# A second mixture of experts: tokens sorted by expert through DRAM, in place of all experts for all tokens

## What is computed

```python
# x = x + _L1_ffn_ref(_layernorm(x), w_gate, w1, w3, w2)
E, H, TOP_K = (8, 256, 2)
xt = x.reshape(-1, embed_dim)
logits = xt @ w_gate
top_logits, sel = jax.lax.top_k(logits, TOP_K)
probs = jax.nn.softmax(top_logits, axis=-1).astype(x.dtype)
h = jax.nn.silu(jnp.einsum('td,edh->eth', xt, w1)) * jnp.einsum('td,edh->eth', xt, w3)
y = jnp.einsum('eth,ehd->etd', h, w2)
yk = y[sel.T, t_idx[None, :], :]
out = jnp.einsum('ktd,tk->td', yk, probs)
```

## Time and profile before

| | |
|---|---|
| median of 3 runs | 2715.28 us (2713.32 to 2717.45) |
| the profiled execution, device time | 2702.93 us |
| its span, first to last instruction | 2701.1 us |
| TensorE busy / its clock, mean | 89% / 0.945 |
| VectorE, ScalarE, GpSimd busy | 71%, 52%, 54% |
| the two `moe1` layers | 1546.2 to 1866.1 us and 2383.2 to 2701.1 us |

### The profile page before, as it was taken

One profiled execution on the slowest core, in us unless ns is written; L12 is line 12 of the kernel. 1 busy time (PEld: TensorE's weight loads), 2 busy tenths in 40 slices (PEclk: granted clock), 3 DMA queues, 4 the chain that ended last, 5 costly groups with the idle time before them and its releaser, 6 DMA issues. The chain is left out here.

```text
span 2701.1 us, 40094 instructions
## 1 busy us (share of the span) xinstructions
PE 2417.3 (89%) x12716; PEld 1529.1 (57%) x12716; DVE 1928.1 (71%) x4454; ACT 1413.1 (52%) x2280; POOL 1453.0 (54%) x1357
## 2 busy tenths in 40 slices
PE   4477997998789889979999989998999999979999
PEld 3344564666756566644444467776444444447777
DVE  6865775775677667756666578887787778758887
ACT  4642454333435533346666455554677677655554
POOL 5924654333365634356666545554776576425554
PEclk8788898998979989999999999998999999989999
DMA  1001111221011022210000021110000000022221
GB/s 48 0 3 29 36 37 57 95 89 56 1 47 42 14 93 91 95 57 1 1 1 1 26 84 64 56 56 32 1 1 1 2 1 1 1 79 68 71 67 44
DMA packets 57513, 104.50 MB, mean 39 GB/s; under 512 B 15192, under 2 KB 30424, under 8 KB 57048
## 3 DMA queue, kind: packets, MB, share of 16 engines
q1 hardware_dynamic: 57304, 101.90, 12.0%
HBM read 86.53 MB, written 2.62 MB: 33 GB/s over the span
## 5 line engine op out<-in xcount | busy, mean ns | idle before, releaser
L4469 POOL TENSOR_TENSOR l_moe1sc<-l_moe1s,l_moe1bcs 128x512 f32<-128x512 f32 x192 | 281.5, 1481 | 223.3 <-ACT l_moe1s L4291 204.0
L2327 DVE TENSOR_REDUCE l_diffneg_max<-psum 128x1 fp32r<-128x512 f32 x512 | 335.3, 685 | 92.1 <-PE psum L2065 84.2
L2242 ACT ACTIVATE l_diffweights<-psum 128x1024 f32<-128x1024 f32 x256 | 262.0, 1026 | 131.6 <-PE psum L2094 130.4
L4291 ACT ACTIVATE l_moe1s<-psum 128x512 f32<-128x512 f32 x256 | 152.5, 597 | 212.2 <-PE psum L851 209.3
L4380 DVE TENSOR_TENSOR x<-l_moe1sc,psum 128x512 f32<-128x512 f32 x256 | 174.6, 682 | 97.6 <-POOL l_moe1sc L4469 57.1
L2065 PE MATMUL psum<-l_diffkz,l_diffQ 128*128 128x512 f32 (+1 forms) x512 | 234.9, 477 | 3.8 <-DVE l_diffneg_max L2327 2.7
L2866 ACT ACTIVATE l_lightswapped<-psum 32x512 f32<-32x512 f32 x304 | 179.0, 589 | 100.9 <-DVE l_lightturned L2958 97.4
L4387 DVE TENSOR_TENSOR l_moe1g_lo<-x,l_moe1g_hi 128x512 fp32r<-128x512 f32 x256 | 221.7, 867 | 0.4 <-ACT l_moe1g_hi L4266 0.2
L1592 DVE TENSOR_REDUCE l_attn0neg_max<-psum 128x1 fp32r<-128x512 f32 x256 | 167.3, 683 | 52.8 <-PE psum L1326 50.1
L1498 ACT ACTIVATE l_attn0weights<-psum 128x1024 f32<-128x1024 f32 x128 | 130.3, 1024 | 120.4 <-PE psum L1348 120.4
L4291 ACT ACTIVATE l_moe0s<-psum 128x512 f32<-128x512 f32 x144 | 85.8, 596 | 200.0 <-PE psum L851 178.1
(11 more groups left out here) (584 smaller groups left out, 6706.4 us busy)
## 6 DMA issues: line engine op xcount, KB each, us to landing
l_moe0bcs<-gate_rows SPq DMA_DIRECT2D x64, 512.0 KB, 4.5
l_moe1bcs<-gate_rows SPq DMA_DIRECT2D x64, 512.0 KB, 3.9
l_attn0Q<-l_attn0q_hi SPq DMA_DIRECT2D x128, 64.0 KB, 2.0
l_moe1w_raw<-in_moe_w SPq DMA_DIRECT2D x20, 256.0 KB, 6.9
l_attn0Q<-l_attn0q_lo SPq DMA_DIRECT2D x64, 64.0 KB, 2.0
l_moe0w_raw<-in_moe_w SPq DMA_DIRECT2D x20, 128.0 KB, 5.1
x<-in_x SPq DMA_DIRECT2D x8, 256.0 KB, 5.0
out<-x SPq DMA_DIRECT2D x8, 256.0 KB, 2.3
```

The costliest lines, as they stand in the source:

```text
L2242: nc.scalar.activation(weights[:, tt, 2 * pair:2 * pair + 2, :], ps[:, S[m % 2]:S[m % 2] + 2, :], ACT.Exp, scale=SCALE).then_inc(act_exp.s ...
L2327: nc.vector.tensor_reduce(neg_max[:, n % 2, st, row:row + 1], ps[:, bank_of(("max", n, b)), :], AXX, ALU.max, negate=True).then_inc(vec_ma ...
L4291: nc.scalar.activation(s[:, n % 2, h, :], ps[:, H1[(n * HT + h) % 2], :], ACT.Silu).then_inc(act_silu.sem, act_silu.step("silu", h))
L4469: nc.gpsimd.tensor_tensor(sc[:, n % 2, h, :], s[:, n % 2, h, :], weights_row(n), ALU.mult).then_inc(pool_sc.sem, pool_sc.step("sc", h))
```

## The change

`moe1` is done by a new function `routed_block`. It works in two chunks of 4 sequences. The head of a sequence is like that of before. After the choice of two experts, TensorE counts with eight small products, against a triangle of ones and a full matrix of ones, how many earlier tokens chose each expert (`ranks`), and VectorE makes from it the row of a DRAM array at which each token stands among those of its expert (`placed`). GpSimd then writes each group of 128 tokens to those rows with an indirect DMA, once for the first choice and once for the second: 8 for a sequence, 32 for a chunk, 64 for a layer (`sort`). A row has 132 numbers: the token, its weight, and the row of the results array to which its result goes. When all of a chunk is counted, VectorE makes a table (`tabled`): for each of 39 tiles its first row and the place of its expert's weights. SyncE pads the end of each expert's region by 8 DMAs with addresses read from that table (`pads`).

Then come the 39 tiles, 128 rows of one expert each, 32 for the 4096 pairs of token and expert and 7 to spare (the number is fixed; spare ones are computed too). A tile: SyncE reads its row number into a register and loads 128x132; TensorE turns it, reads the weights' place into a register, makes one plain float32 product with the turned tile as stationary and 512 columns of weights as moving operand; ScalarE takes the silu of 256 columns; VectorE multiplies it by the token's weight and the other 256 columns in one instruction; TensorE turns the two halves back; ScalarE copies them; TensorE makes two float32 products of 128 columns; VectorE copies the 128x128 result; GpSimd sends it to its rows of `results` by an indirect DMA. The loop over turns (39 + 3 in a chunk) has the steps of successive tiles shifted against each other, and the head and sort of the next chunk's sequences are put in it (`prepare`, 8 turns to a sequence, 2 indirect DMAs in each of 4 turns). The results of a chunk are read back by SyncE and added to `x` twice per sequence on VectorE, in the next chunk's turns or after the last tile.

The rings: 10 tiles loaded, of which each is reused when its result has landed; 4 results; 2 of all else.

```diff
             moe, source = (MOE0, d["moe0_w"]) if self.layer == "moe0" else (MOE1, d["moe1_w"])
             half = FIRST_COLS // 2
-            yield raw[:, 0:half], source[:, moe.w1:moe.w1 + half]
-            yield raw[:, half:2 * half], source[:, moe.w3:moe.w3 + half]
...
@@ rows_kept
-        self.gate.store_rows(sp, 0)
-        sp.wait_ge(self.gate.rows_stored, 16)
+        if self.layer == "moe0":
+            self.gate.store_rows(sp, 0)
+            sp.wait_ge(self.gate.rows_stored, 16)
...
+class Routed:
+    SEQS = 4
+    CHUNKS = NSEQ // SEQS
+    TILES = SEQS * NQ * 2 + 7
...
+            def tile(c, t):
+                n = c * R.TILES + t
+                if n >= SLOTS:
+                    result_out(sp, n - SLOTS)
+                first = sp.value_load(table[0:1, c, ROW_AT + t:ROW_AT + t + 1], min_val=0, max_val=R.ROWS - P)
+                sp.dma_start(xt[:, n % SLOTS, :], core.dram["sorted"][c][bass.ds(first, P), :]).then_inc(tile_loaded[n % SLOTS], 16)
...
+            def up(n, w_at):
...
+                wait(t, act_zt, n, "zt")
+                wait(t, vec_g, n - 2, "g")
+                nc.tensor.matmul(ps[:, H[n % 2], :], zt[:, n % 2, :], w[:, bass.ds(w_at, 4 * P)], start=True, stop=True
+                                 ).then_inc(pe_up.sem, pe_up.step("up"))
...
+                for i in TURNS:                      # TensorE
+                    if i < R.TILES:
+                        at_w[i] = t.value_load(table[0:1, c, W_AT + i:W_AT + i + 1], min_val=0, max_val=7 * R.COLS)
+                        up(n0 + i, at_w[i])
+                    if 0 <= i - 2 < R.TILES:
+                        down(n0 + i - 2, at_w.pop(i - 2))
+                    if i + 2 < R.TILES:
+                        tile_turned(n0 + i + 2)
+                    if 0 <= i - 1 < R.TILES:
+                        g_turned(n0 + i - 1)
+                    prepare(c + 1, i)
...
+            def sort(j, k, q):                       # GpSimd
...
+                p.indirect_dma_start(core.dram["sorted"][chunk_of(j)], bass.IndirectOffsetOnAxis(ap=row_idx[:, j % 2, k * NQ + q:k * NQ + q + 1], axis=0),
+                                     rows[:, j % 2, k, q, :], None).then_inc(sorted_out[j % 2], 16)
+
+            def result(n):
+                wait(p, vec_y, n, "y")
+                p.indirect_dma_start(core.dram["results"], bass.IndirectOffsetOnAxis(ap=xt[:, n % SLOTS, R.DEST:R.DEST + 1].bitcast(U32), axis=0),
+                                     y[:, n % YS, :], None).then_inc(y_out[n % YS], 16)
...
 def moe1_layer(core, ctx, name):
-    moe_block(core, name, MOE1, ExpertWeights(core, ctx, name + "w", "moe1_w", MOE1), "ln", core.x, None, False, store=core.last)
+    routed_block(core, name, store=core.last)
```

More of the change, by code:

```diff
@@ L21 @@
 U32 = mybir.dt.uint32
+I32 = mybir.dt.int32
 ALU = mybir.AluOpType
@@ L367, in loads @@
             half = FIRST_COLS // 2
-            yield raw[:, 0:half], source[:, moe.w1:moe.w1 + half]
-            yield raw[:, half:2 * half], source[:, moe.w3:moe.w3 + half]
             yield raw[:, FIRST_COLS:FIRST_COLS + 8], source[:, 0:8]
             if self.layer == "moe0":
+                yield raw[:, 0:half], source[:, moe.w1:moe.w1 + half]
+                yield raw[:, half:2 * half], source[:, moe.w3:moe.w3 + half]
                 yield f.gain[:, :], d["L0_ffn_g2"].unsqueeze(1)
@@ L393, in pieces @@
             yield raw[:, FIRST_COLS:FIRST_COLS + 8], f.gate[:, 0:8], f.gate[:, 8:16], self.layer == "moe0"
-            yield same(0, FIRST_COLS, self.layer == "moe0")
+            if self.layer == "moe0":
+                yield same(0, FIRST_COLS, True)
     def sync_part(self, sp):
@@ L4497, in _, with scratch @@
                     opening.tokens(p)
+class Routed:
+    SEQS = 4
+    CHUNKS = NSEQ // SEQS
+    TILES = SEQS * NQ * 2 + 7
+    REGION = SEQS * NQ + 1
+    SPARES = 7
+    ROWS = (8 * REGION + SPARES) * P
+    WIDTH = P + 4
+    WEIGHT, DEST = P, P + 1
+    SPARE = 2 * NSEQ * T
+    COLS = 6 * P
+    @staticmethod
+    def scratch(nc, dram):
+        dram["sorted"] = [nc.dram_tensor(f"sorted{c}", (Routed.ROWS, Routed.WIDTH), F32, kind="Internal").ap() for c in range(Routed.CHUNKS)]
+        dram["results"] = nc.dram_tensor("results", (Routed.SPARE + (8 + Routed.SPARES) * P, P), F32, kind="Internal").ap()
@@ L4512, in build @@
     with ExitStack() as ctx:
+        Routed.scratch(nc, dram)
         dram["gate_rows"] = nc.dram_tensor("gate_rows", (NSEQ, 8, T), F32, kind="Internal").ap()
```

452 lines of the change are left out of this document (added).

## The result

Before 2716.36 us (2713.32 to 2725.55), after 2674.54 us (2669.71 to 2678.05): the ratio is 0.9844 [0.9812, 0.9876], 41.8 us less. The forecast was 2690, 25 less. In a later session the same kernel took 2715.3 us against 2718.4, a ratio of 0.999 [0.9969, 1.001]: no gain. Both belong to the result.

The account below looks back on a forecast made before the run. The prediction took the columns TensorE streams as the bound. Its stretches, 72 + 107 + 19 + 87 + 15 + 5 = 305 us and 308 for the last layer, made 613 against 637.8: 2715.3 - 25 = 2690 us, range 2610 to 2850.

Parts of the forecast that it names:

- The price of an indirect DMA: POOL's time per indirect DMA, called t: taken as 1.2 us, between bounds of 0.39 and 5.44.
- Rival (1): POOL's indirect DMA is dearer; from t = 1.32 us on the change is slower than before; chance 0.32.
- rival (3): POOL's indirect DMA is cheap, t at 0.7 to 0.9 us; 2628 us at 0.8; chance 0.20.
- Before the first tile: Layer start to first tile: chunk 0's four sequences pass with nothing beside them, 32 sorts included; 72 us.
- Chunk 0: First chunk's turns: POOL binds at 107 us, as TensorE's 42 turns x 2.0 = 84 would be shorter.
- 71t + 16 + 5: POOL in chunk 0: 39 results and 32 sorts, 16 us for power, scale and iotas, 5 before its first result.
- The boundary: Between the chunks: table, eight pads, landing and first tile in a chain, 19 us with nothing for TensorE.
- Chunk 1: Second chunk: 42 turns x 2.0 us and 3 for DVE's additions, 87 us, plus 5 for TensorE's clock.
- TensorE's saving: Per layer, 78 tiles of 1.55 us make 121 us in place of 268: 147 us of TensorE's work saved.
- Rival (4), the lock: Small DVE steps wait 0.6 us for running indirect DMAs, about 33 us per layer, 2756 us; no separate chance.
- Rival (2): TensorE's turn is dearer, by register read or half clock: at 2.7 us, +36 per layer, 2762 us; chance 0.16.
- Rival (5): The change does not do what it says, though its 39 tiles are fixed and nothing is skipped; chance 0.02.

Follow-up runs that it names:

- e1: The changed kernel with each of the 32 sorts before the first tile issued a second time: 2758.35 us, ratio 1.0162.
- e2: The changed kernel with each of the 32 sorts beside chunk 0's turns issued a second time: 2751.59 us, ratio 1.0148.
- e3: The changed kernel with TensorE reading no register, each tile's weights taken at a fixed place: 2651.81 us, ratio 0.978.
- e4: The changed kernel with 256 columns in place of 512 in the up product: 2656.67 us, ratio 0.9795.
- c2: The changed kernel with the second chunk's table computed in four parts in turns 34 to 37 of chunk 0: 2694.84 us, ratio 0.9917.
- c1: The changed kernel run again, unchanged, in a later session on chip D: 2715.3 us, ratio 0.999.
- e9: The changed kernel with one small POOL instruction behind every indirect DMA of chunk 0, on chip E: 2718.4 us, ratio 1.001.
- c3: The changed kernel with DVE's weights two turns later, token copies two at a time and the second chunk's table early: 2692.29 us, ratio 0.99.

## Why the forecast held, and where it did not

- **The price of an indirect DMA**, the term that decides: 1.2 us taken, 1.26 between starts in the trace, 1.2 by e1. With the bounds 0.39 and 5.44 this was the choice of the nearest row and a reason for somewhat more; it might have missed by half. Rival (1) needed 1.32 and rival (3) 0.9, so both fell by the same row, the first by only 0.06 us: with t = 1.26 and nothing else changed, the forecast's own sum would have left 13 us of its 25. The Trainium skill (DMA: Bandwidth & Descriptors, Latency and other measured facts) had about 1 us until the first byte, which taken as POOL's price would have given 41 us less than the sum. The trace has 0.96 us of busy time, near that figure, but it is the 1.26 between starts that counts.
- **Before the first tile**, 72 against 75.2: the first sort comes at 11.2 us (forecast 12), the sorts are 32 x 1.26 = 40.3, between them lie 5.6 us twice (forecast 6) and 3.2 (3.5). What was too small is t (1.9 us) and the way from the last sort to the first product, 8.1 us where landing, load and turning had 5.6.
- **Chunk 0**, 107 against 113.5. The mechanism was right on chips A and B: e2's 28 added DMAs cost 36.4 us, and e3 and e4 take off only 0.8 to 1.3. The sum "71t + 16 + 5" is off in three places that partly cancel. Only 65 of the 71 DMAs stand in the chunk (65 x 1.26 = 82 where 85 were put); power, scale and iotas take 10.6 in place of 16; and POOL is idle for 21 us in place of 5. Of these, 13.7 lie before the sort stretches begin, 28 us after the first product: there POOL has only 8 results, one power and two scales. The sum treated it as full from the fifth microsecond on.
- **The boundary**, 19 against 19.1, term by term; c2 shows that it is avoidable: 11 us of it go with the table and pads earlier.
- **Chunk 1**, 87 + 5 against 78.1: the read was taken at 0.4 and costs 0.21, so a turn is 1.88 and not 2.0; and the additions on DVE and the clock's start cost next to nothing beside it (granted 0.97 over the stretch; the lower level ends 5 us after the first product). Its 14 us of error cancel most of the two terms that were too small. The three errors -3, -6.5 and +14 made the sum look better than its parts, and that is luck.
- **From the sum to the time.** 15.8 us lie between 2690.3 and 2674.5. The layers explain 8.6 of them (33.6 us less in the traces, 25 forecast); the rest is the spread of executions: 12.4 us were added from profiled execution to median, and after's profiled execution lies only 4.8 under its median. Two of the forecast's signs failed as well: PE was to be busy about 130 us per layer and is 184.8, and chunk 0 was to be 20 us longer than chunk 1 and is 35.
- **TensorE's saving.** 147 us were worked out, the busy time fell by 114. The rows of the tiles' own products are busy for 156.5 us where 121 were forecast. e3 gives the turn's products as 1.64 against 1.55, which is 7 us of it. Of the other 28, at least a part is rows at the lower of the two clock levels: the tiles' rows take 83.4 us in chunk 0 (granted clock 0.89) and 73.1 in chunk 1 (0.97), and the first product of 512 columns behind a pause takes 2.07 us at a granted clock of 0.51, against 1.12 in the middle of chunk 1. How the rest divides was not taken apart. The Trainium skill (TensorE: Matmul & The Clock Gate, Why this matters for your kernels) warns of idle gaps between bursts; the trace agrees, 0.89 in chunk 0 where before had 0.97. It costs busy time; that it does not delay chunk 0, which POOL binds, is argued from e3 and e4 and not shown by itself.
- **Rival (4), the lock.** The counterpart of the instruction of the earlier trace rows, which took 1249 ns in the median there, is short here, but it decides nothing: each of its 16 starts comes 0.03 us behind the end of a power, when POOL has no indirect DMA in progress. What decides are the 578 DVE instructions of the two layers that run while one is in progress. None is more than 0.19 us longer than the shortest of its line and form. Below are the counterpart (first layer), the worst case and the dearest of those that stand in every turn (both layers):
```profile
L4873 DVE TENSOR_SCALAR l_moe1den<-l_moe1e x8: 170/170/172, 1552.0 to 1717.8; 128x4 f32<-128x4 f32 x8
L4909 DVE TENSOR_SCALAR l_moe1tiles_i<-l_moe1whole x4: 171/172/360, 1601.8 to 2551.9; 128x8 int32<-128x8 int32 x4
L4936 DVE SCALAR_TENSOR_TENSOR l_moe1g<-l_moe1s,l_moe1xt,psum x156: 465/472/482, 1623.3 to 2644.3; 128x256 f32<-128x256 f32 x156
```
The port lock that the Trainium skill states (SBUF — State Buffer, Who interferes with whom) fits: there the long instructions in the `moe1` layers end within 0.03 us of a multiplication of POOL that was running when they began. Beside indirect DMAs the trace shows 0.19 us at most, where the rival put 0.6 us for some 55 steps, 33 us per layer.
- **Rival (2)** fell with the turn of 1.88. **Rival (5)** had nothing for it.
- **What no step held**: that one kernel can have two times. On chip D the layers, from the last addition of the layer ahead to their own, take 324.6 and 325.2 us, where before's trace has 321.5 and 315.4 and the changed kernel's first one 302.6 and 300.9. The whole time is the same as before's within its interval. The chance of 0.46 for slower and 0.05 for the same was meant for other reasons; the forecast is right for the chips on which TensorE's results are on time and 25 us too low for the others. The range, 2610 to 2850, holds both.

**Open.** What makes TensorE's results late in three of the five sessions is not known. Shown are its place (only beside the sorts of chunk 0, after some 4 to 13 us of them), its size (22 and 24 us of chunk 0, c1 against the first trace) and two things that it is not: the order of the edits (c1) and an unbroken run of POOL's DMAs (e9, which thins the late results out). The spacing of those DMAs is the same where results are late and where they are not. Whether it needs TensorE's read of registers, or hangs on the number of columns, was not tried on such a chip. One thing goes with it in all 13 traces: the traces with late results lack many records of semaphores, and no other trace does. For the two semaphores that count the sorts' arrivals the first trace has 512 and 511 records in the first 300 us of the layer, c1's 218 and 124; before that layer both have as many as each other (19777 and 19776 of all semaphores). The records are missing from the layer's first sorts on, where no result is late yet. Whether recording and lateness have one cause no run here shows; all ten runs of c1 lie between 2710.65 and 2723.78 us, so the loss is not that of one profiled execution. A version that is best everywhere can't be named either: c3 is 23 us better than the changed kernel on chip D, and was not run on a chip without late results.

## What to carry to other kernels

When a change exchanges work of the busiest engine for a chain of many small steps on others, write the sum as a count times one price per stretch, find the count at which it tips (here 206 indirect DMAs, tipping at 1.32 us), and measure that price first, as the distance between starts and not as busy time. Idle time of an engine is room only if it lies where the added work would stand: POOL's 21 idle us in chunk 0 took up nothing of the 28 DMAs that e2 put there. When a view of waits is summed over a window, look where each wait begins. And compare an edit with its parent in one session: across sessions the same kernel differed by 41 us, twice the edits' own effect.

## What the runs showed of the hardware that was not expected

- An indirect DMA of 128 rows of 528 bytes from GpSimd's queue: 0.96 us busy, 1.26 us from start to start; with a small instruction behind each, 1.37.
- A number read from memory into a register by TensorE's sequencer in every turn costs 0.21 us of the turn of 1.88 (e3), though products are queued ahead of it; SP's read with a DMA behind it 1.08 (8.66 for eight).
- Two bounds 0.2 us apart: taking 0.43 us of product out of a turn gave 0.18, taking the read out 0.21.
- DVE beside indirect DMAs: of 578 instructions that ran while one was in progress, none took more than 0.19 us longer than the shortest of its form.
- Chunk 0 of the changed kernel at 113 us on chip A and at 135.5 and 136.8 on D; the edited ones at 112 to 113 on B where the edit leaves chunk 0 alone, and at 132 to 140 on C and E, with TensorE's results up to 8.4 us late at an engine that is free, 17 to 23 times a layer (12 and 14 in e9's kernel on E).
